# An adaLN attention and mixture-of-experts layer: 77 masked tile stores against 51 direct and 13 merged ones

## What is computed

```python
h = _layernorm(x) * (1 + ca) + sa
x = x + ga * _L0_attn_ref(h, w_in, b_in, w_out, b_out)
h = _layernorm(x) * (1 + cb) + sb
# _L0_ffn_ref:
logits = h @ router_w                       # 14 experts
assignments = argmax(logits); weights = softmax(logits)[assignments]
hid = gelu(einsum('nd,edf->nef', h, w1) + b1)      # f = 256
all_out = einsum('nef,efd->ned', hid, w2) + b2
x = x + gb * (all_out[n, assignments[n]] * weights[n])
```

## Time and profile before

| | us |
|---|---|
| median of 3 runs (625.49 to 626.9) | 626.4 |
| span of the profiled execution | 626.1 |
| expert stage, from the first store (505.5) to the end | 120.6 |
| last VectorE output (tiles 75 and 76) over | 611.8 |
| last store starts | 617.7 |

### The profile page before, as it was taken

One profiled execution on the slowest core, in us unless ns is written; L12 is line 12 of the kernel. 1 busy time (PEld: TensorE's weight loads), 2 busy tenths in 40 slices (PEclk: granted clock), 3 DMA queues, 4 the chain that ended last, 5 costly groups with the idle time before them and its releaser, 6 DMA issues.

```text
span 626.1 us, 11856 instructions
## 1 busy us (share of the span) xinstructions
PE 476.2 (76%) x2529; PEld 269.8 (43%) x2531; DVE 552.7 (88%) x1430; ACT 543.4 (87%) x2310; POOL 498.0 (80%) x655
## 2 busy tenths in 40 slices
PE   5457877887687888787777788788766868989880
PEld 2123333433333333343333344344332548878870
DVE  5899899999999999999999999999999787868660
ACT  2599999999999999999999999999999656757650
POOL 4466777898998999998998989899887664777774
PEclk9556566556756655556656655655655588999886
DMA  6365555555555545554445555655553126676640
GB/s 193 106 184 144 135 136 141 148 149 146 155 151 146 155 139 144 147 148 137 143 135 144 152 158 172 182 164 162 146 156 111 50 90 183 189 205 190 194 124 1
DMA packets 75432, 91.66 MB, mean 146 GB/s; under 512 B 12925, under 2 KB 59043, under 8 KB 75359
## 3 DMA queue, kind: packets, MB, share of 16 engines
q1 hardware_dynamic: 66826, 72.93, 43.6%
q0 software_dynamic: 6560, 16.83, 7.2%
q10 hardware_dynamic: 1976, 1.15, 0.7%
HBM read 58.41 MB, written 33.29 MB: 146 GB/s over the span
## 4 chain that ended last, share of the span: by engine, by line
ACT 47%; POOL 17%; DVE 13%; PE 8%; issue 8%; DMA 5%; ACTq 1%; POOLq 0%; DVEq 0%; SPq 0%
ACT scores L785 46%; DVE neg_max L1218 4%; POOL table L710 3%; PE scores L1052 3%; DMA x_s<-table 2%; POOL xhat L659 2%; PE scores L1061 2%; DMA out_dram<-out_room,ids_s 2%; POOL rstd L642 2%; POOL rest L478 1%; POOL parts L481 1%; POOL out_dram L761 1%; POOL h_scaled L682 1%; DVE w_e L1670 1%; POOL xhat L651 1%
## 5 line engine op out<-in xcount | busy, mean ns | idle before, releaser
L785 ACT ACTIVATE scores<-scores,neg_max 128x256 f32<-128x256 f32 x1024 | 468.5, 864 | 10.9 <-DVE neg_max L1218 10.7
L785 ACT ACTIVATION_READ_ACCUMULATOR scores<-scores,neg_max 128x1 f32 x1024 | 438.3, 624 | 0.0
L1218 DVE TENSOR_REDUCE neg_max<-scores 128x4 f32<-128x1024 f32 x256 | 309.1, 1211 | 6.7 <-PE scores L916 5.9
L916 PE MATMUL scores<-k_stack,q_stack 64*128 64x256 bf16 x1024 | 149.2, 390 | 80.8 <-ACT scores L785 69.2
L916 PEld LDWEIGHTS scores<-k_stack,q_stack 64*128 64x128 bf16 x1024 | 33.9, 106 | 166.1 <-ACT scores L785 121.3
L710 POOL DMA_INDIRECT table<-rows,place_i x64 | 66.1, 1033 | 19.9 <-issue 17.7
L761 POOL DMA_INDIRECT out_dram<-out_room,ids_s x65 | 65.8, 1013 | 19.8 <-issue 15.8
L817 ACT ACTIVATE hid<-scores,w_e 128x128 f32<-128x128 f32 x154 | 48.3, 365 | 22.2 <-PE scores L1052 21.2
L1052 PE MATMUL scores<-x_t,w_e 128*128 128x128 f32 x308 | 52.5, 297 | 1.7 <-ACT x_t L810 1.4
L659 POOL TENSOR_SCALAR xhat<-rows,mv,rstd 128x128 f32<-128x128 f32 x60 | 47.7, 797 | 7.1 <-POOL rstd L642 7.1
L1061 PE MATMUL scores<-w_s,hid 128*128 x308 | 50.1, 288 | 1.1 <-ACT hid L817 0.9
(11 more groups left out here) (178 smaller groups left out, 826.9 us busy)
## 6 DMA issues: line engine op xcount, KB each, us to landing
x_s<-table SPq DMA_DIRECT2D x77, 192.5 KB, 3.0
q_stack<-parts_dram SPq DMA_DIRECT2D x192, 64.0 KB, 2.9
parts_dram<-parts SPq DMA_DIRECT2D x31, 384.0 KB, 3.0
k_stack<-parts_dram SPq DMA_DIRECT2D x186, 64.0 KB, 2.3
mod_b<-mod_rows SPq DMA_DIRECT2D x32, 256.0 KB, 4.3
x_s<-in_x_dram SPq DMA_DIRECT2D x13, 256.0 KB, 4.7
w1x_s<-in_w1x_dram SPq DMA_DIRECT2D x7, 258.0 KB, 4.4
w_s<-in_w_dram SPq DMA_DIRECT2D x7, 256.0 KB, 4.5
```

The source lines that it names most:

```text
L785: last = act.activation(buf[:, k * L:k * L + L], buf[:, k * L:k * L + L], ACT.Exp, bias=neg_max[:, p, n:n + 1], accum_out=exp_sum[:, p, n: ...
L916: last = pe.matmul(scores[:, c, at:at + L], q_stack[p][r, g + j, t * P:t * P + P], k_stack[p][r, g + j, :], start=True, stop=True)
L1218: dve.tensor_reduce(to, scores[:, (PAIRS * b.n + i) % RING, :].rearrange("p (e j m) -> p e j m", e=2, j=2), AX_X, ALU.max, negate=True).th ...
```

## The change

With T = 64, the constants are WHOLE = 51, SHARED = 26 and PACKED = 13. The experts' full tiles are at least 51, whatever the routing. So tiles 0 to 50 are full ones and are stored as before, now with the plain token numbers and without a bounds check. What is left, 13 tiles' worth of rows, is laid out in `packed`, 13 tiles of 128 rows and 129 columns in SBUF (result and token number), into which 26 visits are merged: a visit (tiles 51 to 76) loads 128 rows of one expert from the address at which its rows stand in the partitions that they have in the packed tile. Its result goes into the slot, and one VectorE instruction ands result and number with a mask of the partitions that belong to it (all ones or zero) and ors this into the packed tile. Packed tile k is stored after 14 + k merges. A visit can reach past its expert's last row, so SP writes 128 rows of zeros behind each of the 14 experts' ends (`fill_ends`).

Cut to its core (`shared_*` are 14 functions, called one per step in steps 16 to 29, that work out the visits' expert, first row, packed tile and the edges of their masks; 34 small VectorE instructions on 26 partitions, among them four on 196 and two on 168 columns):

```diff
 def map_reload(j):
-    return EARLY <= j < NT and (j - EARLY) % SLOTS == 0
+    return {EARLY: SLOTS, EARLY + SLOTS: SLOTS, EARLY + 2 * SLOTS: WHOLE - EARLY - 2 * SLOTS,
+            WHOLE: SLOTS, WHOLE + SLOTS: NT - WHOLE - SLOTS}.get(j, 0)
+def merged_by(slot):
+    return slot - WHOLE + E
...
+            def fill_ends():
+                sp.wait_ge(pad_stored, 16 * len(PADS))
+                sp.wait_ge(map_set, 1)
+                for end in load_many(sp, end_row, 0, E, 0, PAD_AT):
+                    sp.dma_start(table[ds(end, P), :], pad_tile[:, :]).then_inc(pad_stored, 16)
-            over_batches(iteration, lambda: None)
+            over_batches(iteration, fill_ends)
...
+                if j == WHOLE:
+                    sp.wait_ge(map_ready, 2)
+                    sp.wait_ge(pad_stored, 16 * (len(PADS) + E))
...
-                need(sp, out_stored[s], 16 * turn)
+                if j - SLOTS < WHOLE:
+                    need(sp, out_stored[s], 16 * turn)
+                else:
+                    sp.wait_ge(merged, j - SLOTS - WHOLE + 1)
...
+                if b.n == 0:
+                    pool.memset(packed[:, :, :], 0).then_inc(pad_set, 1)
...
-                pool.wait_ge(out_ready, j + 1)
-                ids = rows_in[s][:, ID:ROW].bitcast(I32) if j < EARLY else ids_s[:, s:s + 1]
+                if j < WHOLE:
+                    pool.wait_ge(out_ready, j + 1)
+                    ids, rows_of_it = rows_in[s][:, ID:ROW].bitcast(I32), out_s[s][:, :]
+                else:
+                    pool.wait_ge(merged, merged_by(j))
+                    ids, rows_of_it = packed[:, j - WHOLE, D:OUT], packed[:, j - WHOLE, 0:D].bitcast(F32)
...
+            act.dma_start(shared_no[:, 0:2], tile_numbers[WHOLE - EARLY:NT - EARLY, :]).then_inc(w_in_loaded, 16)
...
+            def note_ends():
+                dve.wait_ge(counted, GROUPS)
+                dve.tensor_copy(end_row[:, :], next_row[0:1, :]).then_inc(map_set, 1)
...
+            def load_packed(at, n):
+                packed_at.extend(load_many(dve, packed_now, at, n, 0, PACKED - 1))
...
-                if n >= EARLY:
-                    dve.tensor_tensor(ids_s[:, k:k + 1], rows_in[k][:, ID:ROW].bitcast(I32), mask_i[:, n - EARLY:n - EARLY + 1], ALU.add)
...
+            def merge(n):
+                k, v = n % SLOTS, n - WHOLE
+                dve.wait_ge(out_ready, n + 1)
+                need(dve, merged, v)
+                to = packed[:, ds(packed_at[v], 1), :].rearrange("p o c -> p (o c)")
+                dve.scalar_tensor_tensor(out=to, in0=rows_in[k][:, GW:ROW].bitcast(I32), scalar=mine[:, v:v + 1], in1=to,
+                                         op0=ALU.bitwise_and, op1=ALU.bitwise_or).then_inc(merged, 1)
...
             def tile(j, s, turn):
+                if j == SHARED_TURNED + 2:
+                    take_shared()
...
+                    if n > WHOLE + 1:
+                        merge(n - 2)
```

## The result

The changed kernel takes **631.14 us** (median of 4 runs, 631.01 to 633.3), the kernel before beside it 626.65 (625.49 to 627.38, 4 runs). The ratio is 1.0087, 95% interval 1.0065 to 1.0109: slower by 0.9%, where 622.3 (619.2 to 626.2) had been forecast. The profiled execution took 631.24 us with a span of 629.4.

What follows compares the result with a forecast made beforehand. The prediction took POOL's stores, 1.319 us each, to bound the expert stage. Thirteen fewer save 17.1 us, the wait for the fourteenth merge gives 13 back: 626.4 - 4.1 = 622.3 us, range 619.2 to 626.2.

Steps and rivals of the forecast that it cites:

- The fills, taken at nothing: SP's 14 pad stores, 2.76 MB, ahead of tile 12's load: taken as 0 us, with +3 us as the bad end.
- The slack of 1.6 us: At tile 12, whose output came early for its store on POOL: 1.6 us of lateness was held to be free.
- Rival 2: Slow fill at 192 GB/s: loads 12 to 15 come 4 us late, TensorE stops again; +2.5 to +4 us, chance 0.09.
- The register reads: Reload of SP's registers at tile 67: about 1.0 us, partly beside tile 66's landing, so 0.6 us counted.
- Stores 0 to 50 start 0.5 us earlier: Whole-tile stores keep 1.319 us each; the shorter map work moves their start by -0.5 us, bounds -0.9 and +0.3.
- The bookkeeping is hidden: VectorE's small instructions for shared tiles, steps 16 to 29: 7.9 us, 1.37 us per step, hidden by POOL.
- Rival 3: Bookkeeping starves POOL: VectorE steps 16 to 29 take 2.0 us each, 7.9 us on top, 630 us; chance 0.08.
- Tiles 51 to 76 and the first packed store: POOL idles after store 50 at 583.0 until tile 64's merge; first packed store at 597.7 us.
- rival 6: VectorE's merges in SBUF hold up the packed stores: 0.5 us, or some 2 us each over 12; chance 0.01.
- Twelve intervals of 1.30: The 13 packed stores follow at POOL's own rate: 12 x 1.30 = 15.6 us, last store at 613.6.
- The end 8.4 us behind the last start: From the last store's start to the span's end, 8.4 us as before: end at 622.0.
- rival 4: Shorter end, if POOL's 12.8 us DRAIN pays for stores still in work: up to -3 us, 618 to 619.5; chance 0.06.

Runs made afterwards that it cites:

- experiment 5: Changed kernel with register-table columns from tile 51 on moved one further and the fills put behind the loads of tiles 17 to 43: 621.75 us, ratio 0.9913.
- experiment 1: Changed kernel with the columns of tiles 51 to 76 in both register tables one further, so reads start on 16 bytes: 627.17 us, ratio 0.9995.
- experiment 7: Changed kernel with the old bounds check put back on its 64 output stores: 634.12 us, ratio 1.011.
- experiment 6: Kernel of experiment 5 with the old map's work added back as dummies of the old shapes: 621.86 us, ratio 0.9938.
- experiment 4: Kernel before with only the 14 fills added ahead of tile 12's load, nothing reading what they write: 631.49 us, ratio 1.0069.
- experiment 2: Kernel before with both register tables one column further from tile 12 on, so reads start off 16 bytes: 631.93 us, ratio 1.0076.
- experiment 3: Changed kernel with the 14 fills moved from ahead of tile 12's load to behind the loads of tiles 17 to 43: 626.55 us, ratio 0.9994.

## Why the prediction was wrong

**The fills, taken at nothing.** This is the first step that failed. It cost 4.6 us in the changed kernel, and 4.7 alone in the kernel before. The prediction let the issues end at 519 us (they ended at 519.5) and the data at 520.5, by the 317 GB/s of the earlier trace rows. The data did flow at 301 GB/s in 516 to 520 us, but tile 12's load, issued at 521.54, found the engines still full (a DMA share of 1.00 and more up to 522.5 us) and brought TensorE its rows at 525.77. The larger share was the queue: the prediction held the end of the issues against the map of the kernel before, which it put at 518.5 us, although the change itself brings the map sooner. With no pads ahead, SP reads the registers for tile 12 at 516.4 us and issues its load at 517.59 (experiment 5); behind them it reads at 519.8, and that read takes 1.57 us instead of 1.05. The slack of 1.6 us did not exist. It was worked out for the store of tile 12, but TensorE works in order: it stood in front of tile 12's transpose with the contraction of an earlier tile behind it, so output 7 (519.74 for output 6, then 528.71) and with it POOL stopped at once, and in the trace of before stores 3 to 7 already start 1.07 us behind their outputs, with no slack at all. And what a stop costs behind itself was left out of the base case: tiles 12 and 13 at the 1.2 GHz level, 1.9 to 2.0 us each instead of 1.0. Rival 2 named this second stop of TensorE, with 2.5 to 4 us and a chance of 0.09, but for another reason: it took 192 GB/s, and the rate was not what failed. The bytes were there to be weighed, 2.76 MB in front of the one load for which all engines wait, and so were the issues: 14 of them took 9.8 us, 0.70 each where 0.55 was assumed.

**The register reads.** The prediction had 0.6 us for the one at tile 67 and never spoke of the one at tile 51. They cost 4.0 us together (experiment 1). The diff showed `WHOLE: SLOTS` in place of a regular raster, and the rows showed three durations for reads that all started on 16 bytes; no row of before could give the price of one that doesn't. Bounded from both sides by the rows, a read was 0.3 to 1.2 us. The true value was outside, by a factor of three. What I could have done is to see that the change moves a read to a place that no row covers, on three engines that stand in one chain.

**Stores 0 to 50 start 0.5 us earlier:** too little. With the fills out of the way they start 3.0 us earlier (store 8 at 20.68 from output 0 instead of 23.63), of which 2.5 us are accounted for: the store without bounds check starts 0.5 us sooner (experiment 7), and the short map chain is worth 2 us and not 0.7 (experiment 6, in the trace).

**The bookkeeping is hidden:** right. From store 8 to store 50 the stores are 1.318 us apart in experiment 5, and 1.321 in the kernel before. VectorE's outputs 11 to 25 are 1.35 us apart in experiment 5, near the 1.37 that were worked out. TensorE did wait for it in one place, 1.59 us in front of `turn_shared` for `edges`, in the changed kernel; no store was late for that. Rival 3 did not occur.

**Tiles 51 to 76 and the first packed store:** right in kind. The prediction had it 14.7 us after store 50; in experiment 5 it is 15.3, in the changed kernel 18.9. Tile 66 was turned 7.5 us after store 50 there (586.70, 579.18), where 6.5 was assumed. A step with a merge takes VectorE 1.07 us, under POOL's rate, as assumed. That merges hold up the packed stores (rival 6) is not seen: those are 0.96 us long, like the others of the changed kernel, though VectorE goes on with its copies and merges until 618 us. Rival 6 was also summed wrongly: 2.5 us a store on twelve stores are 30 us, not some 20.

**Twelve intervals of 1.30:** 1.35 in the changed kernel and in experiment 5 (16.2 us). One of them, the first, is 1.99 with VectorE named as releaser, and the eleven others are 1.25 to 1.40, 1.29 on average.

**The end 8.4 us behind the last start:** it is 7.3 in every kernel with packed stores, with the bounds check too, and 8.4 in all three of the old kind that were profiled. So rival 4's shorter end came as well, at 1.1 us, but its reason is not shown. The DRAIN of the earlier trace rows is 11.03 us now against 12.84, yet it is 15.41 and 15.20 us in the two variants of the kernel before (experiments 4 and 2), whose end is 8.4 us like its own. So its length doesn't tell when the end comes, and what took 1.1 us off stays open.

**The whole.** 622.3 was forecast. Without the two costs named first the change measures 621.75 us. That the two agree so well is in part luck: the store start, the map chain and the end were better by some 3 us than the sum had them, counted from output 0, while the profile used for the sum was one whose expert stage began 1.4 us late. In every execution that has both figures the time is 1.8 us above the span, so the profiled one, with a span of 626.1, took about 627.9 us by this estimate and not the median's 626.4.

## What to carry to other kernels

Before anything is put into a DMA queue in front of a load that all engines wait for, add up its issues on the queue, add its bytes to what the engines can move by then, and allow for the slow clock that can follow a stop; a transfer that is needed only later belongs behind the loads. When an edit changes where registers are read from a table, look at the byte at which each read starts: keep it on a multiple of 16, or pad the table. And a change that moves many things at once should be judged by its mechanism only after the two or three incidental costs are taken off: this one lost 0.9% as written, and gains 0.9% with the same stores, fills and reads once the fills stand later in the queue and the table columns one further.

## What the runs showed of the hardware

- A register read (TENSOR_LOAD) of 16 words from SBUF takes SP 1.0 us with the DMA engines not full when it starts on a multiple of 16 bytes of its table and 3.4 us when not; TensorE 1.1 and 3.8 to 4.3, VectorE 1.1 and 3.7 to 4.1.
- Beside the fills aligned reads take longer as well, but not evenly: on SP the read for tile 12 took 1.57 us in the changed kernel, 1.84 in experiment 1 and 1.88 in experiment 4, against 1.03 to 1.06 without fills there. On TensorE it took 2.34 us at 518.1 in the changed kernel and 2.57 in experiment 1, against 1.11 in experiments 3 and 5, but only 1.33 in experiment 4, where the DMA engines were as full (share 1.09).
- An indirect store with a bounds check starts 1.07 to 1.10 us behind the instruction that releases it began, one without 0.56; the shortest intervals between stores are 1.284 and 1.26 us.
- Fourteen DMAs of 197 KB in a row took SP 9.8 us to issue, from 0.33 to 1.79 us each.
- The end of the attention stage varies by 2 us between profiled executions of nearly the same program (output 0 at 502.32 to 504.35), so a single profile of before is a weak base for a difference of one or two us.
